# Two of eight batches convolved by channel on GpSimd, in the head of a state-space and expert kernel

## What is computed

```
xz = jnp.einsum('bld,ed->bel', hidden_states, W_in)
x, z = jnp.split(xz, 2, axis=1)
xp = jnp.pad(x, ((0, 0), (0, 0), (w - 1, 0)))
x = lax.conv_general_dilated(xp, conv_w[:, None, :], (1,), 'VALID', ..., feature_group_count=x.shape[1])
x = jax.nn.silu(x + conv_b[None, :, None])
k = _s4d_kernel(log_dt, log_A_real, A_imag, C_re, C_im, L)
y = jnp.fft.irfft(jnp.fft.rfft(x, n=n) * jnp.fft.rfft(k, n=n), n=n)[..., :L]
y = (y + x * D[None, :, None]) * jax.nn.silu(z)
```

## Time and profile before

| what | us |
|---|---|
| median of three runs | 265.46 |
| the profiled execution | 266.7 |
| its span in the trace | 265.0 |
| head, to the first Toeplitz product | 82.04 |
| loop over the 32 groups | about 49, to 131 |

### The profile page before, as it was taken

How to read it: one execution, slowest core, us unless ns; L and a number is a source line. 1 busy time by engine, 2 the same in 40 slices (tenths; PEclk the granted TensorE clock), 3 DMA queues, 4 the chain that set the end, 5 groups by cost and what they waited for, 6 DMA issues and landing times.

```text
span 265.0 us, 8854 instructions
## 1 busy us (share of the span) xinstructions
PE 243.6 (92%) x2763; PEld 218.1 (82%) x2764; DVE 172.8 (65%) x546; ACT 187.1 (71%) x528; POOL 131.6 (50%) x176
## 2 busy tenths in 40 slices
PE   8999999999999989999988999559989999999970
PEld 4688888888887768888878999549979999999960
DVE  1789993966236657777734778853877666566672
ACT  3979999882999768888835775307668777667740
POOL 6000000300007989999732577777246566557545
PEclk9999999999999999999999999858999999999995
DMA  7659777800199999999284431557755776677510
GB/s 232 156 168 349 285 264 297 326 0 0 42 307 305 339 261 307 332 323 328 59 294 166 117 97 52 161 155 192 239 155 149 209 192 189 189 186 212 185 33 6
DMA packets 54267, 52.06 MB, mean 196 GB/s; under 512 B 4415, under 2 KB 42817, under 8 KB 54114
## 3 DMA queue, kind: packets, MB, share of 16 engines
q1 hardware_dynamic: 51506, 46.65, 58.5%
q0 software_dynamic: 2304, 4.34, 4.6%
q10 hardware_dynamic: 432, 0.79, 0.8%
HBM read 38.14 MB, written 14.07 MB: 197 GB/s over the span
## 4 chain that ended last, share of the span: by engine, by line
PE 71%; DMA 7%; DVE 7%; POOL 6%; issue 5%; ACT 1%; DVEq 0%; SPq 0%; POOLq 0%; ACTq 0%
PE banks L1287 21%; PE banks L1472 8%; PE banks L1365 7%; PE banks L1482 6%; PE banks L1270 6%; PE banks L1375 5%; PE banks L1379 4%; PE banks L1430 3%; DMA X<-dispatched_rows 3%; POOL dispatched_rows L568 3%; DMA out<-X 3%; PE banks L1352 3%; POOL out L576 2%; PE banks L1428 2%; DMA dispatched_rows<-TR,CR 2%
## 5 line engine op out<-in xcount | busy, mean ns | idle before, releaser
L516 POOL TENSOR_TENSOR Wx<-BR,RE 128x384 f32 (+1 forms) x32 | 47.9, 1554 | 29.8 <-PE banks L1287 28.5
L1287 PE MATMUL banks<-Wx,XT 128*128 128x256 f32 x256 | 60.7, 384 | 0.0
L809 ACT ACTIVATE Z<-banks,BR 128x128 f32<-128x128 f32 x156 | 44.5, 368 | 19.1 <-PE banks L1472 19.1
L1287 PEld LDWEIGHTS banks<-Wx,XT 128*128 128x128 f32 x256 | 49.3, 193 | 7.1 <-issue 0.2
L576 POOL DMA_INDIRECT out<-X x39 | 38.5, 987 | 28.4 <-POOL RE L559 12.7
L1472 PE MATMUL banks<-Z 128*128 128x128 f32 x312 | 43.0, 283 | 0.0
L1482 PE MATMUL banks<-BR,Z 128*128 x312 | 41.2, 276 | 1.3 <-DVE X L1211 1.3
L568 POOL DMA_INDIRECT dispatched_rows<-TR,CR x32 | 30.7, 958 | 19.1 <-DVE CR L1136 10.5
L1472 PEld LDWEIGHTS banks<-Z 128*128 128x128 f32 x312 | 39.4, 198 | 0.3 <-issue 0.2
L1482 PEld LDWEIGHTS banks<-BR,Z 128*128 128x128 f32 x312 | 37.8, 192 | 1.5 <-issue 1.4
L1052 DVE TENSOR_TENSOR X<-banks,Z 128x256 f32 (+1 forms) x32 | 20.3, 636 | 9.1 <-PE banks L1379 9.1
(11 more groups left out here) (219 smaller groups left out, 454.9 us busy)
## 6 DMA issues: line engine op xcount, KB each, us to landing
TR<-kernel_rows SPq DMA_DIRECT2D x32, 512.0 KB, 6.1
Z<-w SPq DMA_DIRECT2D x39, 256.0 KB, 3.4
dispatched_rows<-TR SPq DMA_DIRECT2D x3, 2310.0 KB, 8.5
X<-dispatched_rows SPq DMA_DIRECT2D x39, 66.0 KB, 2.9
XT<-hidden_t SPq DMA_DIRECT2D x10, 256.0 KB, 3.0
RE<-decay_and_turns SPq DMA_DIRECT2D x2, 1024.0 KB, 7.5
BR<-w SPq DMA_DIRECT2D x1, 2048.0 KB, 8.1
dispatched_rows<-TR SPq DMA_DIRECT2D x1, 1848.0 KB, 7.6
```

Of the source, the lines that this page charges most:

```text
L516: nc.gpsimd.tensor_tensor(BC[:, k, 0:LAGS, :].rearrange("p m (s r n) -> p (m s) r n", s=STRIPS, r=2), Btab[:, :, :, :, :, one].rearrange(" ...
L809: last = nc.scalar.activation(HT[:, j, c * P:c * P + P], bank[UP_BANKS[j]][:, c * P:c * P + P], ACT.Relu, bias=B1[:, bass.ds(experts[j] * ...
L1287: last = mm(bank[X_BANKS[k]][:, j * CHAN:(j + 1) * CHAN], XT[:, slot, at:at + CHUNK], Wx[:, tap, :], start=(tap == 0), stop=(tap == TAPS - 1))
```

## The change

Batches 2 and 4 (`TURNED`) leave the folded-tap path. For each, `project_channels` makes the four gate products, and then the x part once and the other way round: 128 channels by 512 tokens, two products of 128x512. ScalarE copies both to SBUF (`keep_channels`), and GpSimd does the taps there (`convolve_channels`): for each half of the channels a scaled copy with the bias, and for three more taps a scaled copy and a sum, shifted by a token each. `turn_channels` then turns the result back, token by channel, by eight TensorE transposes of 128x128 per batch into the x banks, and VectorE copies it to `X` without a bias.

`c_turns` moves from ScalarE to GpSimd, ahead of the convolutions, and its tables move from `BR` to the end of `TR`. The product of the output table stays with VectorE. The last lag's absolute value moves from ScalarE to VectorE, and the lags' order is 3, 2, 1. The order of the projections, their banks and the biases is new. The `Kx` zeros come after the output table, and the first Toeplitz load waits for the second batch's turns too, since that batch's tables lie in `TR`.

GpSimd's queue after its first constants, before: it waits for the table and sets constants.

The diff, cut to what is spoken of:

```
-LAG_ORDER = (3, 1, 2)
+LAG_ORDER = (3, 2, 1)
 X_BANKS, Z_BANKS = (4, 5, 0, 1), (2, 3, 6, 7)
+TURNED = (2, 4)
+X_ORDER = (0, 1, 2, 3, 6, 7, 10, 4, 5, 11, 12, 13, 8, 9, 14, 15)
...
-        turnsC = BR[:, 0:GROUPS * KLEN].rearrange("p (g j) -> p g j", g=GROUPS)
-        wholeC = BR[:, GROUPS * KLEN:GROUPS * KLEN + 16 * KLEN].rearrange("p (g j) -> p g j", g=16)
+        turnsC = TR[:, T_SLOTS * GH * CHUNK - GROUPS * KLEN:].rearrange("p (g j) -> p g j", g=GROUPS)
+        wholeC = TR[:, 1948:1948 + 16 * KLEN].rearrange("p (g j) -> p g j", g=16)
+        by_channel = [(BR[:, 0:1024], BR[:, 1024:2048], BR[:, 2048:3072]),
+                      (TR[:, 1948:2972], TR[:, 2972:3996], TR[:, 4608:5632])]
+        by_channel = [[part.rearrange("p (h l) -> p h l", h=2) for part in parts] for parts in by_channel]
...
             sp.wait_ge(s_kd, 16)
+            sp.wait_ge(s_a, x_place(9))
...
+            def c_turns(half):
+                for g in range(half * 16, half * 16 + 16):
+                    last = nc.gpsimd.tensor_scalar(turnsC[:, g, :], jrow[:, :], sm[:, TURNS, g:g + 1],
+                                                   sm[:, PHI, g:g + 1], ALU.mult, ALU.add)
+                last.then_inc(s_cl, 1)
+            def convolve_channels(c):
+                given, sums, scaled = by_channel[c]
+                made = c * 14
+                def weight(h, tap):
+                    return taps[:, h, tap:tap + 1]
+                pool.wait_ge(s_uc, c * 2 + 2)
+                for h in range(2):
+                    nc.gpsimd.tensor_scalar(sums[:, h, :], given[:, h, :], weight(h, TAPS - 1), weight(h, TAPS),
+                                            ALU.mult, ALU.add).then_inc(s_tap, 1)
+                for tap in (2, 1, 0):
+                    late = TAPS - 1 - tap
+                    done_before = made + 2 + (2 - tap) * 4
+                    for h in range(2):
+                        pool.wait_ge(s_tap, done_before + h - 1)
+                        nc.gpsimd.tensor_scalar(scaled[:, h, late:], given[:, h, 0:SEQ - late], weight(h, tap), None,
+                                                ALU.mult).then_inc(s_tap, 1)
+                    for h in range(2):
+                        pool.wait_ge(s_tap, done_before + h + 1)
+                        last = nc.gpsimd.tensor_tensor(sums[:, h, late:], sums[:, h, late:], scaled[:, h, late:], ALU.add)
+                        last.then_inc(s_tap, 1)
+                pool.wait_ge(s_tap, made + 14)
+                nc.gpsimd.memset(scaled[:, 0, 0:1], 0.0).then_inc(s_acc, 1)
+            pool.wait_ge(s_pad, 2)
+            pool.wait_ge(s_cwb, 2)
+            pool.wait_ge(s_phi, 1)
+            c_turns(0)
+            c_turns(1)
+            pool.wait_ge(s_tw, 16)
+            convolve_channels(0)
             pool.wait_ge(s_c, 2)
+            nc.gpsimd.memset(Kx[:, :, :], 0.0).then_inc(s_kx0, 1)
+            convolve_channels(1)
...
-                    if i == 0:
-                        act.wait_ge(s_bt, 2)
+                    if i != 1:
+                        act.wait_ge(s_bt, i + 2)
                     elif q:
                         act.wait_ge(s_bw, i * 4 + 4)
                         nc.scalar.activation(Btab[:, LAG_ORDER[i] - 1, :, 0, :, :].rearrange("p s n g -> p s (n g)"), rows, ACT.Abs)\
                           .then_inc(s_ba, 1)
                     else:
-                        act.wait_ge(s_ba, i)
+                        act.wait_ge(s_ba, 1)
...
-            def c_turns(half):
-                act.wait_ge(s_phi, 1)
-                for g in range(half * 16, half * 16 + 16):
-                    last = nc.scalar.activation(turnsC[:, g, :], jrow[:, :], ACT.Identity, scale=sm[:, TURNS, g:g + 1],
-                                                bias=sm[:, PHI, g:g + 1])
-                last.then_inc(s_cl, 1)
+            def keep_channels(c):
+                if c:
+                    act.wait_ge(s_ct, 2)
+                for h in range(2):
+                    act.wait_ge(s_u, c * 2 + h + 1)
+                    nc.scalar.activation(by_channel[c][0][:, h, :], bank[X_BANKS[h]], ACT.Copy).then_inc(s_uc, 1)
             keep_z(0, 0)
+            keep_z(0, 1)
             act.wait_ge(s_rowl, 32)
             state_decay(2)
-            c_turns(0)
-            keep_z(0, 1)
-            c_turns(1)
             keep_z(0, 2)
+            c_decay(range(EARLY, GROUPS))
             keep_z(0, 3)
-            c_decay(range(EARLY, GROUPS))
             keep_z(1, 0)
-            act.wait_ge(s_const, 3)
+            keep_z(1, 1)
+            keep_channels(0)
+            act.wait_ge(s_const, 2)
             c_sines(0)
-            keep_z(1, 1)
+            state_sines(0)
+            keep_z(1, 2)
             c_sines(1)
-            keep_z(1, 2)
-            state_sines(0)
             keep_z(1, 3)
             keep_z(2, 0)
             keep_z(2, 1)
+            keep_channels(1)
             state_sines(1)
...
                 n = i * 4 + k
-                dve.wait_ge(s_a, n + 1)
+                dve.wait_ge(s_a, x_place(n))
                 b = bass.ds(i * 2 + k // 2, 1)
-                tt(x_pairs[:, :, k % 2, :, b].rearrange("p c j b -> p j (c b)"),
-                   bank[X_BANKS[k]][:, :].rearrange("p (j c) -> p j c", j=2),
-                   cbias[:, :].unsqueeze(1).to_broadcast([P, 2, CHAN]), ALU.add).then_inc(s_xb, 1)
+                into = x_pairs[:, :, k % 2, :, b].rearrange("p c j b -> p j (c b)")
+                summed = bank[X_BANKS[X_HOME[n]]][:, :].rearrange("p (j c) -> p j c", j=2)
+                if i * 2 + k // 2 in TURNED:
+                    nc.vector.tensor_copy(into, summed).then_inc(s_xb, 1)
+                else:
+                    tt(into, summed, cbias[:, :].unsqueeze(1).to_broadcast([P, 2, CHAN]), ALU.add).then_inc(s_xb, 1)
...
             state_turns(0, 0)
-            state_turns(0, 1)
             bias(0, 1)
             bias(0, 2)
+            state_turns(0, 1)
             c_fraction(0)
             bias(0, 3)
-            bias(1, 0)
             state_turns(0, 2)
             c_fraction(1)
+            state_turns(1, 0)
+            bias(1, 2)
+            bias(1, 3)
+            c_table(0)
+            state_turns(1, 1)
+            c_table(1)
+            bias(2, 2)
+            bias(1, 0)
             bias(1, 1)
-            bias(1, 2)
-            c_table(0)
-            bias(1, 3)
-            c_table(1)
-            dve.wait_ge(s_c, 2)
-            state_turns(1, 0)
-            state_turns(1, 1)
-            bias(2, 0)
-            bias(2, 1)
-            bias(2, 2)
             state_turns(2, 0)
+            bias(2, 3)
             state_turns(2, 1)
-            bias(2, 3)
             bias(3, 0)
-            dve.wait_ge(s_const, 2)
+            state_turns(2, 2)
+            dve.wait_ge(s_kx0, 1)
...
+                nc.vector.tensor_copy(Kx[:, j:j + 1, 0:CHUNK], backwards(X_BANKS[2], j * CHUNK + CHUNK - 1, 1))\
                   .then_inc(s_kx, 1)
             dve.wait_ge(s_kx, 2)
             tt(Kx[:, :, CHUNK - 1], Kx[:, :, CHUNK - 1], dskip[:, :], ALU.add).then_inc(s_kx, 1)
-            for k in range(1, 3):
-                bias(3, k)
+            bias(3, 1)
+            bias(2, 0)
+            bias(2, 1)
+            bias(3, 2)
...
+            def project_channels(c):
+                batch = TURNED[c]
+                slot = batch % A_BATCH
+                batch_loaded(batch)
+                for n in (batch * 2, batch * 2 + 1):
+                    wait_past(pe, s_z, n - 3)
+                    project_gates(n % 4, 0, slot)
+                    project_gates(n % 4, 1, slot).then_inc(s_za, 1)
+                for h in range(2):
+                    if c:
+                        pe.wait_ge(s_uc, h + 1)
+                    pe.wait_ge(s_xb, x_place(h))
+                    mm(bank[X_BANKS[h]], Win[:, h * P:h * P + P], XT[:, slot, XPAD:], start=True, stop=True).then_inc(s_u, 1)
+            def turn_channels(c):
+                pe.wait_ge(s_acc, c + 1)
+                for n in (TURNED[c] * 2, TURNED[c] * 2 + 1):
+                    if n == 8:
+                        pe.wait_ge(s_kx, 2)
+                    elif n == 4 or n == 5:
+                        pe.wait_ge(s_uc, n - 1)
+                    x_home_free(n)
+                    for j in range(2):
+                        at = (n % 2 * 2 + j) * CHUNK
+                        for h in range(2):
+                            last = nc.tensor.transpose(bank[X_BANKS[X_HOME[n]]][:, j * CHAN + h * P:j * CHAN + h * P + P],
+                                                       by_channel[c][1][:, h, at:at + CHUNK], ident[:, :])
+                    last.then_inc(s_a, 1)
...
+            for n in range(4):
+                project(n)
+            project_channels(0)
+            project(6)
+            project(7)
+            project_channels(1)
+            project(10)
+            pe.wait_ge(s_const, 2)
+            turn_channels(0)
+            project(11)
```

(33 more changed lines are left out.)

88 lines of the change are left out of this document (42 added, 46 removed).

## The result

The changed kernel took 288.21 us (median of four runs, 287.62 to 291.53), the kernel before 265.63 beside it: 1.087 times as long, with an interval of 1.078 to 1.096. The forecast was 273.0 in a range of 257 to 280: the sign was right, the size not. The profiled execution took 288.18 us with a span of 286.4, against 265.0 before.

A forecast was written before the change was run, and what follows sets the result against it. TensorE was taken to bound the head; afterwards GpSimd's new work plus VectorE's blocking would delay it, the head ending at 89.6 instead of 82.04, 7.5 us later. Added to the median 265.46 that gave 273.0, range 257 to 280.

The forecast's parts named there:

- The step that failed: Prices of GpSimd's new head work: 0.25 us a turn, 0.55 a one-input operation, 1.2 a sum; 31.7 us in all.
- The hold: In the head, GpSimd and VectorE's large operations exclude each other both ways through shared SBUF ports; 21.1 plus 5.4 us charged.
- The sum: End of the second batch's convolution on GpSimd: start, its own work and VectorE's operations added up, 79.9 us.
- a cost of the lower clock: TensorE in the head, coming out of its wait for the first batch, runs at the 1.2 GHz level: 1.8 us.
- the gap ahead of the first turns: TensorE waits before its first eight transposes back, about 15 us, ended by GpSimd; the sign for the main step.
- the Toeplitz loads' shorter lead: Loads ahead of the loop: lead of 8.6 us instead of 10.2, taken as free (at most 1.6).
- ScalarE's relief: ScalarE loses two blocks of turns, 6.26 us each, and gains four copies; off the chain, so worth nothing by itself.
- the third: Rival: both engines wait and GpSimd is slow, sums 2.07 us, turns 0.35, 53 us of work: 294, half way 283; chance 0.08.
- The second: Rival: both engines wait but GpSimd is fast: 262.9 us, or 269.4 with sums of 1.05; chance 0.15.
- The first: Rival: GpSimd doesn't wait for VectorE, or the operations don't meet; head up to 8.2 us earlier, 257.2 to 259; chance 0.27.
- TensorE alone bounds the head: The part before the first Toeplitz product, ending at 82.04, is TensorE's own work; dropping taps saves at most 8.2 us.

The follow-up runs named there:

- The benches: The kernel before, with GpSimd and VectorE instructions added behind its last store, timed alone and side by side; 3.95 us of VectorE cost GpSimd 1.4 to 2.9 us.
- no_taps_order: The changed kernel without GpSimd's shifted products and sums, biases and gate copies queued ahead of what waits for the output table's turns: 263.89 us.
- the one-batch version: Against the kernel before: only batch 2 by channel, two-scalar products, output table's turns on ScalarE, turning back behind step 12: 268.8 us against 266.64, 1.008 times.

## Why the prediction was wrong

**The step that failed** is "I take 0.25 for a turn and 0.55 for a one-input operation, a little above what only writes". A turn took 0.445 undisturbed (32 x 0.195 = 6.2 us more), a one-scalar product 1.55 (12 x 1.0 = 12.0 more), a two-scalar first product 0.755 (4 x 0.2 = 0.8), a sum 1.235 where 1.2 was taken (0.4). GpSimd's own work is 31.7 + 19.4 = 51.1 us. Rows that only write have no price for arithmetic; the range should have had two to three times theirs as a likely end. The Trainium skill's page "GPSIMD Engine Reference", section 3.1, has 769 ns measured for 512 elements in a tight loop: the two-scalar product has that length, the one-scalar one takes twice that, and no row of the page tells the forms apart.

**The hold** was right in kind and too large: 26.5 us of VectorE were charged in full; GpSimd's queue lasted 69.3, so its waits are 69.3 - 51.1 = 18.2. The benches show part of why: no form pays VectorE's time in full there. But the price isn't one for all. With some 10 us of the table's work gone, GpSimd's waits fell by 9.9, to 8.3: the table's large instructions cost about what the forecast charged, and the three lags of state turns, 16.2 us by the forecast, only about half. Why these differ was not tested. VectorE's own lengthening was forecast at up to one instruction of GpSimd; the output table's product, 2.302 in the earlier trace rows, lasted up to 4.99, about two of GpSimd's sums more. The Trainium skill's page "SBUF — State Buffer", section "Who interferes with whom", has the first to start hold the other off for its whole instruction. The sums come near to it (both last 10 us beside each other; one after the other would be 7.61 + 3.95 = 11.6), and the PSUM readers without effect agree; beside turns and two-scalar products VectorE was hardly held at all (4.00 and 4.61 against 3.95).

**The sum**: 20.96 + 51.1 + 18.2 = 90.2, where 21.7 + 31.7 + 26.5 = 79.9 was forecast: 10.3 us. Behind it 11.4 us instead of 9.7: the forecast has a cost of the lower clock behind TensorE's first wait and none behind its second, where the granted clock was 0.54 (eight turns 1.97 instead of 1.04, a step's products 2.45 instead of 1.89): most of the 1.7. The head is thus 12.0 us later than forecast, and the part behind the head gave 1.9 that the forecast had at nothing, 13.9 us in all: 274.2 became 288.2. The prices alone were 19.4 us too low; that the hold was 8.3 too high hid part of it, by luck.

**Right**: the gap ahead of the first turns has the cause that was named; the sums cost 1.2; the lengths depend on VectorE; the Toeplitz loads' shorter lead (9.2 us) cost nothing that the trace shows. That the gap's length, 15.11 for 15, agrees too is chance, since both its ends were some 6.5 us late, for different reasons. GpSimd was done at 68.97 instead of 62.4. TensorE, forecast at the turns at 47.7, was there at 54.06, although in this execution it had been through projection 2 at 19.7 and not at 23.5. It had stood twice, 6.5 us together, for biases queued behind VectorE's wait for GpSimd's turns, and lost some 3 us more at a granted 0.50 behind the first stand. The forecast named such a wait for the kernel rows alone. With those biases put ahead (`no_taps_order`) TensorE was at the turns at 47.97. That ScalarE's relief is worth nothing by itself is not shown: in both versions with the turns back on ScalarE, TensorE waited 7.6 to 7.8 us for a copy in ScalarE's queue.

**The rivals**: the third, slow GpSimd at 283 to 294, came true in size, by other terms (it had slow sums; the sums were right and the products slow). The second's work with sums of 1.05 adds up to 27.9, not 28.1, which changes nothing. The first, at 257 to 259, could not have come true at that price: with no tap work at all the time was 270.2, and 263.9 with the queues reordered. And that TensorE alone bounds the head holds only for a small gain: in the kernel before ScalarE's last preparation for the loop ended at 80.8, 1.3 us ahead of the loop, and in the one-batch version ScalarE stopped TensorE, which was through at 77.9.

## What to carry to other kernels

Before work is moved to an engine whose arithmetic the trace doesn't show, price the very form of instruction in a bench of a few lines; two forms that compute the same can differ by twice. When an engine is given work that others wait for, list what stands behind each of these waits in its queue: here biases and gate copies, which fed the bound, stood behind waits for the new work. Work taken off the bound pays only down to the next engine's end, here ScalarE's.

## What was not expected of the hardware

- On GpSimd a product with one scalar took 1.55 us for 512 columns, the same with a second scalar added 0.76; with immediate numbers 1.49 and 0.62, a copy 0.61.
- From 128 to 512 columns the two-scalar form grew from 0.44 to 0.76 us only.
- A sum of 510 columns, one input read two columns off the other, took 1.09 us against 1.26 with both at the same place.
- Sums of GpSimd and VectorE's two-tensor products, six of each side by side, lasted 1.6 to 1.7 us each, where alone they took 1.26 and 0.66; beside VectorE reading PSUM GpSimd's took what they take alone (the two-scalar products 4.75 us for six).
